# Fifth coefficient of the composed convolution in two products, and a new order of GpSimd's low parts

## The reference

```python
# x: (64 batches, 64 channels, 1024); cond_512: (64, 128)
x = x + S4(conv_stack(x, cond_512, weights...))        # first pass
x = x + FFN(conv_stack(x, cond_512, weights2...))      # second pass
# conv_stack: four modulated, demodulated convolutions of 3 taps, each weight scaled per batch
#   s = style @ mw.T + mb; w = SCALE*w*s; w = w * rsqrt(sum(w*w) + eps)
#   'same', 'upsample' (stride 2, then blur), 'same', 'downsample' (blur, then stride 2)
# S4: causal convolution of length 1024 along time, plus D*u
# FFN: x @ W_base.T + b, and a rank-16 LoRA over 8 experts, the best 2 by a router, softmax gates
```

## Time and profile before

| | |
|---|---|
| median of 3 runs | 1326.04 us (1325.16 to 1326.46) |
| profiled execution | 1323.71 us, span 1321.9 us |
| mean granted TensorE clock | 0.994 of full speed |
| PE / DVE / ACT / POOL busy | 97% / 78% / 64% / 69% of the span |

### The profile page before, as it was taken

One profiled execution on the slowest core, in us unless ns is written; L12 is line 12 of the kernel. 1 busy time (PEld: TensorE's weight loads), 2 busy tenths in 40 slices (PEclk: granted clock), 3 DMA queues, 4 the chain that ended last, 5 costly groups with the idle time before them and its releaser, 6 DMA issues.

```text
span 1321.9 us, 23280 instructions
## 1 busy us (share of the span) xinstructions
PE 1278.5 (97%) x8214; PEld 1221.7 (92%) x8214; DVE 1037.5 (78%) x2311; ACT 840.7 (64%) x1772; POOL 916.5 (69%) x730
## 2 busy tenths in 40 slices
PE   3789999999999999999999999999999999999999
PEld 3589899899889999999999989999999999999998
DVE  7877878777877778877878888787887878787872
ACT  4587777778777877777465554655656465565640
POOL 6468887666677777667767666767777767767752
PEclk9799999999999999999999999999999999999999
DMA  3234454444554655454452432534434252433433
GB/s 131 78 108 134 134 135 134 134 134 134 134 134 134 144 146 144 130 154 124 82 156 78 132 103 78 144 90 123 111 103 131 78 156 78 138 97 117 118 85 89
DMA packets 86277, 158.23 MB, mean 120 GB/s; under 512 B 26633, under 2 KB 48402, under 8 KB 86034
## 3 DMA queue, kind: packets, MB, share of 16 engines
q1 hardware_dynamic: 84898, 154.79, 42.1%
q10 hardware_dynamic: 1264, 1.96, 0.5%
HBM read 93.79 MB, written 33.56 MB: 96 GB/s over the span
## 4 chain that ended last, share of the span: by engine, by line
PE 85%; DVE 5%; POOL 3%; ACT 2%; issue 2%; DMA 1%; SPq 0%; DVEq 0%; POOLq 0%; ACTq 0%
PE psum L1897 28%; PE psum L1899 27%; PE psum L1898 27%; PE psum L2028 2%; DMA vm_f<-vv 1%; POOL xs_l L964 1%; DMA w3T<-in_w_dram 1%; POOL vs_l L959 1%; DVE vm_l L1627 0%; PE psum L289 0%; POOL as_l L991 0%; DVE a_l L1654 0%; ACT xin L1165 0%; DVE a_f L1659 0%; DVE c_l L1611 0%
## 5 line engine op out<-in xcount | busy, mean ns | idle before, releaser
L1897 PE MATMUL psum<-wt_h,u_h 128*128 128x386 f32 (+1 forms) x760 | 261.2, 344 | 0.0
L1899 PE MATMUL psum<-wt_h,u_l 128*128 128x386 f32 (+1 forms) x760 | 258.2, 340 | 0.0
L1898 PE MATMUL psum<-wt_l,u_h 128*128 128x386 f32 (+1 forms) x760 | 258.0, 339 | 0.0
L1677 DVE STREAM_TRANSPOSE turned<-vbuf 32x256 f32<-32x256 f32 x480 | 209.1, 436 | 7.9 <-ACT vbuf L1238 0.7
L939 POOL TENSOR_TENSOR vbuf<-vbuf 128x512 f32<-128x512 f32 x64 | 97.7, 1526 | 159.0 <-ACT vbuf L1252 159.0
L953 POOL TENSOR_TENSOR vm_f<-vm_f 128x512 f32<-128x512 f32 x64 | 82.8, 1293 | 138.3 <-DVE vm_l L1627 138.0
L1245 ACT ACTIVATE vbuf<-psum,tabs 128x512 f32<-128x512 f32 x128 | 105.2, 821 | 114.1 <-PE psum L1899 110.6
L1897 PE MATMUL psum<-a_h,vm_h 128*128 128x256 f32 x512 | 148.4, 290 | 3.2 <-ACT vbuf L1245 3.0
L1898 PE MATMUL psum<-a_l,vm_h 128*128 128x256 f32 x512 | 146.1, 285 | 0.0
L1899 PE MATMUL psum<-a_h,vm_l 128*128 128x256 f32 x512 | 145.8, 285 | 0.0
L1897 PEld LDWEIGHTS psum<-wt_h,u_h 128*128 128x128 f32 x760 | 143.5, 189 | 1.1
(11 more groups left out here) (336 smaller groups left out, 4174.6 us busy)
## 6 DMA issues: line engine op xcount, KB each, us to landing
vm_f<-vv SPq DMA_DIRECT2D x256, 112.0 KB, 4.5
xin<-in_x_ph_dram SPq DMA_DIRECT2D x32, 512.0 KB, 5.0
xr<-in_x_row_dram SPq DMA_DIRECT2D x32, 512.0 KB, 4.1
x1d<-xr SPq DMA_DIRECT2D x64, 256.0 KB, 3.3
xin<-x1d SPq DMA_DIRECT2D x32, 512.0 KB, 4.7
xr<-x1d SPq DMA_DIRECT2D x64, 256.0 KB, 5.6
xo<-in_b_base_dram SPq DMA_DIRECT2D x32, 512.0 KB, 6.0
out_dram<-xo SPq DMA_DIRECT2D x31, 512.0 KB, 2.9
```

What stands on the lines that cost most here:

```text
L1677: ins = V.transpose(u_f[to, :, :].rearrange("p b (k n) -> p b k n", n=P)[:, :, :, frm], v3[frm, :, :].rearrange("p b (k n) -> p b k n", n= ...
L1897: nc.tensor.matmul(to, stat_h, mov_h, start=first_ and n == 0, stop=False, skip_group_check=True)
L1898: nc.tensor.matmul(to, stat_h, mov_l, start=False, stop=False, skip_group_check=True)
L1899: ins = nc.tensor.matmul(to, stat_l, mov_h, start=False, stop=end, skip_group_check=True)
```

## The change

The fifth coefficient's low part is put into the HIGH half of `c1_h`'s third block, beside the high part in the LOW half, from tile `STACKED` = 35 on. A table `r_h[:, 0]` holds the even-tap rows' high part in both halves, so one matmul gives high by high plus low by high; `r_l[:, 0]` holds the low part in LOW and zero in HIGH, so the second gives high by low. `step2` then has eight matmuls and not nine. DVE makes `c1_l` with four instructions per tile (two of 64 partitions by 64 columns, two of 128 by 128) for two of 128 by 192. In turn 32 ACT copies the tables (three instructions of 64 partitions by 320 columns) and DVE clears the zero half. GpSimd's `inputs_low` is cut in two: `z_l` goes ahead of the wait for `vm_lo`, right behind L1007; and `pair_sums_low(i+1)` comes at the end of turn i, ahead of the two differences, and no longer at the head of turn i+1.

```diff
+STACKED = TILES + 3
@@ GpSimd
-            def inputs_low(g):
+            def even_inputs_low(g):
                 pool.wait_ge(z_hi, nth(g))
-                G.tensor_tensor(z_l[:, :, :], xin[:, :, 0:H:2], z_h[:, :, :].bitcast(F32), ALU.subtract)
+                G.tensor_tensor(z_l[:, :, :], xin[:, :, 0:H:2], z_h[:, :, :].bitcast(F32), ALU.subtract).then_inc(z_lo, 1)
+
+            def differences_low(g):
                 pool.wait_ge(in_hi, at(g))
...
             def body(i):
-                if here(i):
+                if here(i) and not halved(i + 1):
                     pair_sums_low(i)
...
+                if halved(i + 2):
+                    even_inputs_low(i + 2)
+
                 if any(edges(i, n) for n in (2, 3)) or 2 <= i <= 6:
                     pool.wait_ge(v3_val, at(i))
+                    if halved(i + 2):
+                        pool.wait_ge(z_lo, nth(i + 2))
...
                     if halved(i + 2):
-                        inputs_low(i + 2)
+                        pair_sums_low(i + 1)
+                        differences_low(i + 2)
@@ ACT
+            def last_tap_tables():
+                act.wait_ge(step2_done, TILES)
+                act.wait_ge(r_lo, 2)
+                for half in HALF:
+                    A(r_h[half, 0, :, :], r_h[LOW, 1, :, :].bitcast(F32), ACT.Copy)
+                A(r_l[LOW, 0, :, :], r_l[LOW, 1, :, :].bitcast(F32), ACT.Copy).then_inc(rx_ready, 1)
...
                 if turn_is(i, 6):
                     r_high(1)
+                if turn_is(i, TILES):
+                    last_tap_tables()
@@ DVE
+            def composed1_stacked(g):
+                c, t = place(g)
+                ve.wait_ge(c1_hi, at(g))
+                for b in range(2):
+                    scalar = tabs[:, c, T_S3, batch(t, b)]
+                    V.scalar_tensor_tensor(out=c1_h[HIGH, 2, b, :], in0=ps_taps[LOW, 2, b, :], scalar=scalar[LOW],
+                                           in1=c1_h[LOW, 2, b, :].bitcast(F32), op0=ALU.mult, op1=ALU.subtract)
+                    ins = V.scalar_tensor_tensor(out=c1_l[:, 0:2, b, :], in0=ps_taps[:, 0:2, b, :], scalar=scalar,
+                                                 in1=c1_h[:, 0:2, b, :].bitcast(F32), op0=ALU.mult, op1=ALU.subtract)
+                ins.then_inc(c1_lo, 1)
...
+                if turn_is(i, TILES):
+                    ve.wait_ge(step2_done, TILES)
+                    V.memset(r_l[HIGH, 0, :, :].bitcast(F32), 0.0).then_inc(rx_ready, 1)
@@ PE, step2
+                if g == STACKED:
+                    pe.wait_ge(rx_ready, 2)
-                for n in range(3):
+                for n in range(2 if stacked(g) else 3):
                     ins = product(ps_step[:, C * n:C * (n + TAPS)],
...
+                if stacked(g):
+                    taps = c1_h[:, 2, :, :].rearrange("p b o -> p (b o)")
+                    for t in (r_h, r_l):
+                        ins = nc.tensor.matmul(ps_step[:, 2 * C:2 * C + TAPS * C], taps, t[:, 0, :, :].rearrange("p d o -> p (d o)"),
+                                               start=False, stop=t is r_l, skip_group_check=True)
```

More of the change, by code:

```diff
@@ L576, in program @@
     in_scaled = sem("in_scaled")
+    rx_ready = sem("rx_ready")
     ms_sum, ms_hi, ms_lo = sem("ms_sum"), sem("ms_hi"), sem("ms_lo")
-    z_hi, dif_set, dif_begin = sem("z_hi"), sem("dif_set"), sem("dif_begin")
+    z_hi, z_lo, dif_set, dif_begin = sem("z_hi"), sem("z_lo"), sem("dif_set"), sem("dif_begin")
     y_sum, shared_done, shared_out = sem("y_sum"), sem("shared_done"), sem("shared_out")
@@ L699, in turned_f, with stacked @@
         return u_f if by_blocks(g) else ps_x
+    def stacked(g):
+        return here(g) and g >= STACKED
     def first(g):
@@ L1605, in scaled1 @@
                 ins.then_inc(y1_lo, 1)
+            def composed1_stacked(g):
[8 more added lines that the diff above has]
+                ins.then_inc(c1_lo, 1)
             def composed1(g):
+                if stacked(g):
+                    composed1_stacked(g)
+                    return
                 c, t = place(g)
```

## The result

| | before | changed |
|---|---|---|
| median | 1325.21 us (1323.29 to 1326.46, 22 runs) | 1327.14 us (1325.13 to 1330.19, 22 runs) |
| ratio, 95% interval | | 1.0017, [1.0011, 1.0023], that is +2.3 us, [1.5, 3.0] |
| profiled execution | 1323.71 us, span 1321.9 | 1329.3 us, span 1327.5 |

The prediction was +2.2 us and 1328.2. The two profiled executions lie 5.6 us apart; against its own median, before's is short and the changed kernel's long. At 589 us from the start of the span, ahead of everything that the change touches, PE of the changed kernel is already 1.7 us behind (the same matmul, counted from the first, starts that much later). So sums over whole profiles overstate the change; distances inside one turn don't have this 1.7 in them.

A forecast was written before the change was run, and what follows sets the result against it. PE, 97% busy, was taken as bound, so a saved matmul counts only if no next wait replaces it. Terms: -6.7 (`third`) +6.1 (evacuation) +0.9 and +0.8 (`hw`) +1.1 (tables) = +2.2 us, 1328.2; range 1317.5 to 1333.

The forecast's parts named there:

- `third`: Head of `third`, where PE waits for `vs_l`: with `vs_l` earlier on POOL the gap goes, -6.7 us.
- L1718 behind `z_l`: DVE's SBUF-to-SBUF copy in the router: held until 0.03 us after POOL's `z_l` ends, 0.89 us late each turn.
- The first rival: DVE's copy L1718 passes beside `z_l` without being held: -7.9 us in all, 1318.1 us; 18%.
- `c1_l`: DVE's making of `c1_l`: four instructions cost 1.11 us against 0.73 for two, 0.38 us more a tile.
- The evacuation: ACT's evacuation of `pair(0)` before `pair(1)`: starts 0.29 us late behind DVE's transpositions, 0.21 lost a turn, +6.1 us.
- `hw`: PE's weight load of `hw`: DVE 0.15 us late, 0.03 lost a turn (+0.9 us), and 0.8 more in turn 40.
- Tables: Turn 32: ACT's three table copies stand ahead of an evacuation without margin, once +1.1 us.
- The third rival: The bias row's transfer comes too late for POOL in half the turns: 7.3 us on top, 1335.5 us; 14%.

The follow-up runs named there:

- Experiment 5: Kernel before with only `vs_l` moved ahead of `z_l` and the differences; nothing stacked, no tables, `z_l` not early: 1319.62 us, ratio 0.9966.
- experiment 1: Changed kernel with `z_l` moved back behind `vs_l`, stacking and early `vs_l` kept: 1319.65 us, ratio 0.9957 to the kernel before.
- experiment 3: Changed kernel with the copy of the experts' indices (L1718) made by ACT instead of DVE: 1318.67 us, ratio 0.9950 to the kernel before.
- experiment 6: Kernel before with only the indices' copy (L1718) moved to the end of `router_begin`, where L1007 has just begun: 1442.0 us against 1324.08, one execution.
- experiment 7: Changed kernel with `z_l` moved back behind `vs_l` and the tables copied in turn 33, not 32: 1318.79 us, ratio 0.9950 to the kernel before.
- experiment 4: Kernel before with stacking alone (eight matmuls, four instructions for `c1_l`, tables), GpSimd in its old order: 1326.13 us, ratio 1.0007.

## Why the prediction was right

By its own steps:

- **`third`**: forecast -6.7, measured -6.7, and the gap is gone in every turn, turn 41 too. Experiment 5 asks for this alone: its trace has the same -6.7, its times -4.5 [-5.8, -3.2].
- **L1718 behind `z_l`**: forecast 0.89 us late and ending 0.03 behind it. In the timeline DVE's way from the copy's start to that of `vm_l` is 1.98 us (938.70 to 940.68) where it was 1.12, so +0.86. The first rival is out: experiments 1 and 3 each undo this meeting (1 moves `z_l`, 3 the copy) and stand 8.0 and 8.9 us below the changed kernel (5.7 or 6.6, and 2.3). The Trainium skill (SBUF — State Buffer, "SBUF: two separate sides") says that of a GpSimd instruction and a VectorE one in a two-port mode or with two SBUF inputs, the one that starts first keeps the shared ports for its whole instruction and the other fully blocks. The traces agree, with 2.44 us for 8 elements in experiment 6.
- **`c1_l`**: mis-sized. Forecast +0.38 a tile; its start to that of the transpositions is 1.33 us (942.52 to 943.85) where it was 0.76, so +0.57. An instruction of 128 columns costs a step of 0.37 (942.81 to 943.18), where I had taken 0.308, its share of the busy time in the earlier trace rows; one of 64 columns costs 0.29, where I had taken 0.249 by a straight line through 128 and 192 columns. So the four cost 0.2 more than the 1.11 of the forecast. The upper bound of 0.6 held it. Between `vm_l` and `c1_l` 0.06 came back, so the transpositions are 1.37 late, not 1.27.
- **The evacuation**: forecast ACT 0.29 late and 0.21 lost a turn, +6.1 in all. Measured from the copy's start, ACT is 0.37 late (7.89 us for 7.52) and follows DVE by 0.04, not 0.06. PE loses 10.8 at `pair(1)` and has 4.0 less to do in `step2`: +6.8. In a normal turn the second matmul of `pair(1)` starts 1.714 us behind the first of `step2`, where it was 1.437 (medians), so 0.28 is lost and not 0.21.
- **`hw`**: forecast +1.7 with turn 40. Found: +2.8. Turn 40 has 0.9 of it (0.8 forecast). The others have 1.9 and not 0.9, 1.1 of it in turns 34, 35 and 38, the last two with a late bias row. In turn 40 the gap is 1.36 us where it was 0.47, counted between starts less their steps (the number in brackets counts from the end of the weight load before):

```profile
777.18 0.14 PEld L2245 LDWEIGHTS psum<-ident,hw 128*128 128x128 f32 x1 [1.47 <-DVE hw L1767]
```

- **Tables**: forecast +1.1, seen 0.9 (0.80 of gap and 0.10 between the first two matmuls behind it).
- **The third rival** is partly at work: in 12 of the turns 33 to 61 L1015 waited for the bias row, against 2 before (57 and 58). One of them, turn 52:

```profile
1051.44 2.68 POOL L1015 TENSOR_TENSOR xo<-xr,xo 128x1024 f32<-128x1024 f32 x1 [0.42 <-DMA xo<-in_b_base_dram]
...
1053.93 0.23 DVE L1757 CAST topf<-topi 128x8 f32<-128x8 uint32 x1
...
1054.08 1.31 POOL L990 TENSOR_TENSOR z_l<-xin,z_h 128x512 fp32r<-128x512 f32 x1
...
1055.10 1.45 DVE L1666 TENSOR_TENSOR vm_l<-vm_f,vm_h 128x512 fp32r<-128x512 f32 x2
```

  Here the copy started inside L1015, was held only until its end (0.23 us), and went ahead of `z_l`, whose start was late instead. In four turns (45, 52, 56, 58) this made the turn shorter, about 22.7 us; the others took 22.9 to 23.7. The twelve together took 276.5 us, as twelve normal turns of 23.04 would. So a late transfer works both ways, and did not decide.

With the tables the profile has +4.1 us (3.2 and 0.9) where the forecast had +2.2, and the times have +2.3 [1.5, 3.0]. One execution isn't good for tenths here: experiments 1 and 7 have the same instructions in turns 34 to 62, and their traces took 642.19 and 643.33 us for them. The forecast's small total is a difference of two large terms. That it came within 0.1 us is luck: the evacuation and `hw` cost more in the trace than forecast. That both terms are there is not luck: with the meeting undone the gain stands alone (-5.7 and -6.6 in experiments 1 and 3), and the distance from there to the changed kernel (8.0 and 8.9) is the loss.

## What to carry to other kernels

Idle time of GpSimd is free only if no VectorE instruction that shares its ports falls into it: list those beside the gap first, the tiny SBUF-to-SBUF copies too. A matmul that is saved counts only if the next wait is covered by something else; here it covered an evacuation, and a matmul moved up from a later product restored the cover (-6.6 to -9.3 us). When two edits each lengthen the same engine's way, add their delays before you compare with its margin: each alone left the evacuation on time here.

## What the runs showed that I had not expected

- A copy of 8 elements is held for 2.44 us by a GpSimd instruction of 2.68 us (experiment 6), while the router's 128x1 operations, `RECIPROCAL` and the instruction with an input in PSUM (`hw`) keep their 0.15 to 0.35 us beside `z_l` (experiment 3).
- How long the copy is held can be worked out: it is longer by what the running GpSimd instruction has left at its start, less 0.14 us. Over the 30 held copies of the changed kernel and the 30 of experiment 6 this last number lies between 0.135 and 0.148.
- It works in the other direction too: `vs_l` on GpSimd took 2.25 us for 1.3 when `u_l` had begun on VectorE. In experiment 6 the waits at `third`, half of them from this, cost more than the hold-up that was the experiment's aim. The kernel before has it once: in turn 41 `vs_l` took 2.26 us (from 779.30) beside `u_l` (from 779.07). That is about half of the 2.0 us of this turn, which the forecast took over without a reason.
- Taking work from PE alone (experiment 4) gave nothing at 97% busy.
- In experiment 6 a quarter of the price (29 of 118 us) was TensorE's clock, which fell to its lower level behind the waits, and not the waits themselves.
